# Early expert tiles: row loads without padding and release waits between them, scatters in strict turn, and a reordered hand-over

## The chip, the core and the metric

The kernel runs on one core of a Trainium2 chip. The time is that of one execution on the device, in microseconds (us); lower is better. A profile is a separate execution taken by the hardware profiler, with a span from its first to its last instruction.

## The reference

The input x is 8 sequences of 512 tokens with 256 channels, in float32. `_layernorm` is a plain normalisation over the channels, without weights.

```python
# 1: a state-space layer as a long convolution, in a residual branch
xn  = _layernorm(x)
K   = s4d_kernel(log_A_real, A_imag, C_re, C_im, log_dt, length)
y   = irfft(rfft(xn, 2*length) * rfft(K, 2*length))[:, :length]
r   = xn + y + xn * D
a   = layernorm(r) * ln_w + ln_b
x   = x + _layernorm(a)
# 2: a mixture of 8 experts, the best 2 for each token
u      = _layernorm(x)
z      = layernorm(u) * ln_g + ln_b
probs  = softmax(z @ rW + rb)
w      = top-2 of probs, divided by their sum
hid    = gelu(z @ W1[e] + b1[e])            # exact gelu, 256 -> 512
outs   = hid @ W2[e] + b2[e]                # 512 -> 256
x      = x + _layernorm(u + sum over e of outs * w[e])
```

## The kernel before

The work has three stages. In the first (0 to about 240 us) the batches go one by one through the convolution, and each token is normalised and given its two experts. In the second the 8192 token rows are worked on in 71 tiles of 128 rows. In the third (from about 519 us) the summed rows are read back, normalised and stored.

**Rows in DRAM.** For each batch GpSimd (POOL) scatters 1024 rows (`scatter`, 8 indirect DMAs) into `z_rows`, one region for each expert; a row holds its 256 values, its token number, its second expert and a logit difference. The result of a tile is weighted and added to `y_rows` by one indirect DMA that accumulates (`scatter_y(t)`); two tiles of one expert never share a token, two tiles of different experts can. So the addition of a tile may not be under way together with that of a tile of another expert.

**Early tiles.** The tiles 0 to 13 (`FIRST` = 14) take rows of the first five batches only, in the order of the experts (`first_tiles` on VectorE, DVE). Tiles 14 to 70 take the rest and begin again with expert 0; their addresses come from `count`, `share` and `tell`, which DVE runs inside the tile loop. Because the last tile of an expert reads beyond its rows, eight blocks of `zpad` are written behind the regions (`pad(e)`) before tile 14 is loaded.

**One tile.** SyncE (SP) loads the rows (`load_z`, with the address from `tab`) into `z_in`, two buffers. TensorE (PE) transposes them (`transposes`), multiplies by W1 (`first_layer`), transposes the hidden values (`turned`) and multiplies by W2 (`second_layer`). ScalarE (ACT) does `scaled`, `tilt` (a tanh), `settle`, `high`, `gelu` and `weigh`; DVE does `row`, `bias`, `low` and `output`. Each engine's order is written out by hand; in round i PE does `transposes(i+2)`, `first_layer(i+1)`, `turned(i)`, `second_layer(i-1)`. `load_z(t)` waits until tile t-2 has been transposed (`tz_mm`) and read by `row` (`dest_ready`). `yw` has six buffers, so `weigh(t)` waits for the scatter of tile t-6.

**Release.** `y_out0` and `y_out1` count the landed scatters of even and odd tiles. `scatter_y(t)` always waits for tile t-2's. For tile t-1 SP reads a number from `order`, which DVE writes in `turns`: all earlier scatters of the other parity, less one if tile t has the expert of tile t-1. SP waits for this many and raises `released`, for which POOL waits. SP does so in its one queue, between the loads:

```python
for t in range(FIRST, TILES):
    load_z(t)
    release(t - 6)
```

so `load_z(21)` stands behind `release(14)`, and in general the load of tile t+1 behind `release(t-6)`.

**The hand-over.** In the last step of stage one (`n == B`) each engine prepares tiles 0 and 1 beside the choice of experts for the last batches (`choose`, `place` on DVE; `rank`, `logits` on PE). `spin(n, bank)` is n products whose results nobody reads. The last batch is scattered by POOL ahead of `scatter_y(2)` (`EARLY` = 2).

## Time and profile before

| what | value |
|---|---|
| median of 3 runs | 565.91 us (563.12 to 567.77) |
| the profiled execution's own time | 563.68 us |
| its span | 561.6 us |
| mean granted TensorE clock | 0.93 of 2.4 GHz |
| PE, DVE, ACT, POOL busy | 80%, 79%, 67%, 48% |

Busy shares are means over stages with different limits. A timeline row gives start, length, engine, line, operation, shapes, count, and in brackets the idle time ahead of it with what ended it. PE's ends are modelled from its pipeline. Times in the rows below are us from the start of the span; tiles and their scatters are numbered from 0, and the transposes of tile 14 are those at 315.97 us.

### The profile page before, as it was taken

What the parts mean: (1) busy time and instruction counts of PE and PEld (TensorE: products, weight loads), DVE (VectorE), ACT (ScalarE), POOL (GpSimd) and SP (SyncE); (2) the same over time, 40 slices, a digit from 0 to 9 for tenths busy, and PEclk for the clock granted to TensorE, in tenths of its full rate; (3) what the DMA queues carried; (4) which work ended last, traced back from release to release, by engine and by line L of the source; (5) the groups of instructions that cost most, each with busy time, mean ns of one, the idle gap of its engine ahead of it and who ended that gap; (6) DMA issues with size and microseconds to landing.
All of it is one profiled execution on the core that took longest, in us unless ns stands there. A gap on an engine that the chain in (4) does not pass through costs nothing.

```text
span 561.6 us, 11667 instructions
## 1 busy us (share of the span) xinstructions
PE 449.8 (80%) x2730; PEld 387.5 (69%) x2730; DVE 442.2 (79%) x1492; ACT 377.1 (67%) x928; POOL 268.0 (48%) x195
## 2 busy tenths in 40 slices
PE   0296899967999978588668999999999999999100
PEld 0146888846988867257557898999999999998100
DVE  6999795999898988874858777887888878887282
ACT  6992864446666657866535777777777777776184
POOL 0000359444566877564274344445444445444365
PEclk9997999999999997688978999999999999999655
DMA  6302730042224366496245457545544444444596
GB/s 168 134 1 100 298 127 1 0 131 77 104 95 171 141 218 207 121 350 207 49 128 96 76 97 176 80 75 85 84 79 78 77 77 77 77 77 53 146 403 269
DMA packets 47615, 70.35 MB, mean 125 GB/s; under 512 B 7616, under 2 KB 37184, under 8 KB 47040
## 3 DMA queue, kind: packets, MB, share of 16 engines
q1 hardware_dynamic: 34256, 51.82, 27.7%
q0 software_dynamic: 13296, 17.80, 19.0%
q8 instruction: 26, 0.43, 0.3%
q14 instruction: 37, 0.30, 0.2%
HBM read 37.90 MB, written 31.70 MB: 124 GB/s over the span
## 4 chain that ended last, share of the span: by engine, by line
PE 47%; DVE 25%; ACT 11%; issue 6%; DMA 5%; POOL 2%; SPq 2%; another core or an unknown queue 1%; DVEq 1%; POOLq 0%; ACTq 0%
PE psum L1487 15%; PE psum L1511 14%; PE psum L1497 5%; PE psum L1407 3%; DVE ws L934 3%; DMA yr<-y_rows 2%; PE psum L1471 2%; DVE st L739 2%; PE psum L1365 2%; ACT dump L652 2%; PE psum L1354 2%; PE psum L1355 1%; DVE o L1147 1%; ACT ws L589 1%; PE psum L1378 1%
## 5 line engine op out<-in xcount | busy, mean ns | idle before, releaser
L1316 POOL DMA_INDIRECT y_rows<-yw,dst x71 | 113.0, 1591 | 141.3 <-SPq L398 86.6
L1487 PE MATMUL psum<-ws,z_hl 128*128 x426 | 121.6, 422 | 6.2 <-issue 3.2
L1511 PE MATMUL psum<-ws,h_hl 128*128 x852 | 116.4, 286 | 0.6 <-DVE h_hl L1100 0.6
L1511 PEld LDWEIGHTS psum<-ws,h_hl 128*128 128x128 f32 x852 | 104.0, 189 | 0.8 <-issue 0.8
L1487 PEld LDWEIGHTS psum<-ws,z_hl 128*128 128x128 f32 x426 | 77.7, 196 | 22.2 <-issue 8.9
L1272 POOL DMA_INDIRECT z_rows<-zn,pos x64 | 71.0, 1110 | 27.4 <-issue 17.1
L597 ACT ACTIVATE z_f<-psum,gb 128x128 f32<-128x128 f32 x142 | 57.2, 453 | 17.5 <-issue 7.5
L634 ACT ACTIVATE hg<-hb 128x512 f32<-128x512 f32 x71 | 44.9, 633 | 31.1 <-DVE hb L1094 30.1
L1407 PE MATMUL psum<-yf,it 128*128 128x256 f32 x256 | 59.2, 387 | 2.6 <-DVE r L1121 2.6
L1081 DVE CAST z_hl<-z_f 128x256 fp32r<-128x256 f32 x71 | 21.0, 296 | 48.7 <-PE psum L1487 31.9
L1378 PE MATMUL psum<-pm,ft 128*128 128x256 f32 x256 | 58.2, 382 | 0.4 <-DVE tmp L920 0.2
L627 ACT CAST h_hl<-psum 128x512 fp32r<-128x512 f32 x71 | 41.6, 585 | 24.1 <-PE psum L1497 19.4
L1407 PEld LDWEIGHTS psum<-yf,it 128*128 128x128 f32 x256 | 49.0, 194 | 9.7 <-POOL yf L1259 3.1
L1378 PEld LDWEIGHTS psum<-pm,ft 128*128 128x128 f32 x256 | 47.8, 190 | 7.2 <-issue 1.1
L1094 DVE TENSOR_TENSOR hb<-psum,b1r 128x512 f32<-128x512 f32 x71 | 48.6, 684 | 2.4 <-PE psum L1487 1.4
L1100 DVE TENSOR_TENSOR h_hl<-psum,h_hl 128x512 fp32r<-128x512 f32 x71 | 48.3, 681 | 2.3 <-ACT h_hl L627 2.0
L1497 PEld LDWEIGHTS psum<-ident,hg 128*128 128x128 f32 x284 | 36.4, 144 | 10.6 <-issue 0.6
L1497 PE MATMUL psum<-ident,hg 128*128 128x128 f32 x284 | 43.6, 277 | 0.2 <-DVE h_hl L1100 0.2
L1257 POOL TENSOR_TENSOR yf<-yf,tmp 128x512 f32<-128x512 f32 x16 | 24.4, 1525 | 39.4 <-DVE o L1147 29.6
L1265 POOL TENSOR_TENSOR pm<-xn 128x512 f32<-128x512 f32 x8 | 10.3, 1286 | 67.2 <-ACT xn L492 67.2
L607 ACT ACTIVATE yw<-y_sb,wt 128x256 f32<-128x256 f32 x71 | 35.7, 503 | 4.5 <-DVE y_sb L1111 3.2
L1471 PE MATMUL psum<-ident,z_in 128*128 128x128 f32 x142 | 27.9, 279 | 8.4 <-DMA z_in<-z_rows 4.2
(222 smaller groups left out, 841.2 us busy)
## 6 DMA issues: line engine op xcount, KB each, us to landing
z_in<-z_rows SPq DMA_DIRECT2D x71, 129.5 KB
w_raw<-in_dram SPq DMA_DIRECT2D x16, 512.0 KB, 5.9
xs<-in_dram SPq DMA_DIRECT2D x8, 512.0 KB, 5.4
x_dram<-xs SPq DMA_DIRECT2D x8, 512.0 KB
y_rows<-zn SPq DMA_DIRECT2D x8, 512.0 KB, 3.5
yr<-y_rows SPq DMA_DIRECT2D x8, 512.0 KB, 7.3
out_dram<-acc SPq DMA_DIRECT2D x7, 512.0 KB, 5.0
b1r<-in_dram SPq DMA_DIRECT2D x8, 256.0 KB
```

Source lines behind the costliest of these rows:

```text
L597: last = nc.scalar.activation(z_f[:, k], ps_z[:, k], ACT.Identity, bias=gb[:, 1, k:k + 1], scale=gb[:, 0, k:k + 1])
L627: nc.scalar.copy(h_hl[t % 2][:, 0], ps_t).then_inc(sem("h_high"), 1)
L634: nc.scalar.activation(hg[t % 2][:, :], hb[:, :], ACT.Gelu).then_inc(sem("hg_ready"), 1)
L1094: V.tensor_tensor(hb[:, :], ps_h[t % 2], b1r[:, bass.ds(e, 1)].rearrange("p a f -> p (a f)"), ALU.add).then_inc(sem("hb_ready"), 1)
L1100: V.tensor_tensor(h_hl[t % 2][:, 1], ps_t, h_hl[t % 2][:, 0].bitcast(F32), ALU.subtract).then_inc(sem("h_split"), 1)
L1272: pool.indirect_dma_start(z_rows, bass.IndirectOffsetOnAxis(ap=pos[row.par][:, i // 4, i % 4:i % 4 + 1], axis=0), zn[buf(row.b)][:, i % 4] ...
L1316: pool.indirect_dma_start(y_rows, bass.IndirectOffsetOnAxis(ap=dst[t % 8][:, 0:1], axis=0), yw[t % 6][:, :], None, compute_op=ALU.add).the ...
L1378: last = TE.matmul(fw[u][c][:, k], ft[:, c, t, kt * P:(kt + 1) * P], pm[row.b][:, c, t], start=t == 0, stop=t == 1)
L1407: last = TE.matmul(iv[c][:, j * H:(j + 1) * H], it[:, c, k, j * P:(j + 1) * P], yf[row.par][:, c, k], start=k == 0, stop=k == KT - 1)
L1487: last = TE.matmul(ps_h[q], z_hl[q][:, a, k], w_at(e, c, k * F, F), start=n == 0, stop=n == 5)
L1497: last = TE.transpose(ps_t[:, k], hg[t % 2][:, k * P:(k + 1) * P], ident[:, :])
L1511: last = TE.matmul(ps_y[q], h_hl[q][:, a, k], w_at(e, c, 1024 + k * H, H), start=n == 0, stop=n == 11)
```

## The change

Five things are edited. `release` and `pad` leave the loads of the tiles below 14: no early tile is released by SP, and the pads are issued two at a time behind the loads of tiles 9 to 12. In exchange POOL itself waits, ahead of each early scatter, until all scatters of the other parity have landed, whatever the expert. `turns` isn't run for the early tiles. ACT runs a Gelu on one number ahead of the last batch's normalisation, and `enlarge` of the last batch ahead of `gelu(0)`. PE transposes tile 1 ahead of `rank` and does six more spins; DVE splits expert 6's weights after `choose` and `row(1)`; SP loads tiles 2 and 3 earlier among the stores. The scatters take their indices from `row_of` itself, and the copy into `dst` goes.

```diff
--- before.py
+++ after.py
@@ -152,7 +152,6 @@
     tab = at("tab", [1, 2, TILES + 1], I32, c0 + 4960)
     d_rep = at("d_rep", [P, H], F32, o0 + 72 * KB)
     tab_e = at("tab_e", [P, TILES + 1], F32, c0 + 5952)
-    dst = [at(f"dst{i}", [P, 1], U32, o0 + 71 * KB + 256 + 32 * i) for i in range(8)]
     row_of = at("row_of", [P, TILES + 1], U32, o0 + 71 * KB + 736)
     half = [at(f"half{i}", [P, 1], F32, o0 + 71 * KB + 32 * i) for i in range(3)]
     lean = [at(f"lean{i}", [P, 1], F32, o0 + 71 * KB + 96 + 32 * i) for i in range(3)]
@@ -413,33 +412,34 @@
                 sp.dma_start(b1r[:, e], rep(b1[e])).then_inc(sem("in_b"), 16)
             for e in range(E):
                 sp.dma_start(b2r[:, e], rep(b2[e])).then_inc(sem("in_b"), 16)
-            store_rows(6, 7)
-            sp.wait_ge(sem("x1_ready"), B)
-            sp.dma_start(x1_dram[:, B - 1], xs[B - 1][:, :, :]).then_inc(sem("x1_stored"), 16)
-            load_z(2)
-            sp.wait_ge(sem("zn_ready"), B)
-            sp.dma_start(y_tok[:, B - 1], zn[buf(B - 1)][:, :, 0:H]).then_inc(sem(f"zn_stored{buf(B - 1)}"), 16)
-            load_z(3)
+            for b in (6, 7):
+                sp.wait_ge(sem("x1_ready"), b + 1)
+                sp.dma_start(x1_dram[:, b], xs[b][:, :, :]).then_inc(sem("x1_stored"), 16)
+                if b == 7:
+                    load_z(3)
+                sp.wait_ge(sem("zn_ready"), b + 1)
+                sp.dma_start(y_tok[:, b], zn[buf(b)][:, :, 0:H]).then_inc(sem(f"zn_stored{buf(b)}"), 16)
+                if b == 6:
+                    load_z(2)
             sp.wait_ge(sem("x1_stored"), 16 * B)
             for b in (4, 5):
                 sp.wait_ge(sem(f"scattered{buf(b)}"), sent(b))
                 sp.wait_ge(sem(f"zn_stored{buf(b)}"), sent(b) // 8)
             load_expert(sp, 7)
-            load_z(4)
-            load_z(5)
-            for t in range(6, FIRST):
+            for t in range(4, FIRST):
                 load_z(t)
-                if t > 6:
-                    release(t - 6)
-                if t == 6:
+                if t == 9:
                     sp.wait_ge(sem("pad_set"), 1)
-                pad(t - 6)
+                if 9 <= t < 13:
+                    pad(2 * (t - 9))
+                    pad(2 * (t - 9) + 1)
             sp.wait_ge(sem("pads"), 16 * E)
             for b in (5, 6, 7):
                 sp.wait_ge(sem(f"scattered{buf(b)}"), sent(b))
             for t in range(FIRST, TILES):
                 load_z(t)
-                release(t - 6)
+                if t - 6 >= FIRST:
+                    release(t - 6)
                 if 20 <= t < 23:
 
                     b = B - 1 - (t - 20)
@@ -668,6 +668,8 @@
                     measure(cur)
                 if n == B:
                     scaled(1)
+
+                    nc.scalar.activation(wt[5][:, :], eps[:, 0:1], ACT.Gelu)
                     renormalise(cur)
 
             act.wait_ge(sem("kf_mm"), 1)
@@ -682,8 +684,8 @@
             tilt(0)
             tilt(1)
             settle(0)
+            enlarge(Row(B, -1))
             gelu(0)
-            enlarge(Row(B, -1))
             for i in range(TILES + 2):
                 if i + 2 < TILES:
                     scaled(i + 2)
@@ -1018,7 +1020,6 @@
                 V.tensor_scalar(tab_e[:, 0:FIRST], tf_h[:, 0], float(E - 1), None, ALU.min)
                 do(V.scalar_tensor_tensor(tf_h[:, 2], tf_h[:, 0], float(REGION), iot[:, 1, 0:FIRST], ALU.mult, ALU.add))
                 do(V.scalar_tensor_tensor(tf_h[0:1, 3], tf_h[0:1, 1], -float(P), tf_h[0:1, 2], ALU.mult, ALU.add))
-                turns(1, FIRST, tf_h)
                 V.tensor_copy(tab[:, 0, 0:FIRST], tf_h[0:1, 3]).then_inc(sem("tab_ready"), 1)
 
             def count():
@@ -1107,7 +1108,6 @@
                 if t >= 2:
                     dve.wait_ge(sem("yw_ready"), t - 1)
                 gate(dve)
-                V.tensor_copy(dst[t % 8][:, :], row_of[:, t:t + 1])
                 V.tensor_tensor(y_sb[t % 2][:, :], ps_y[t % 2], b2r[:, bass.ds(e, 1)].rearrange("p a f -> p (a f)"),
                                 ALU.add).then_inc(sem("y_ready"), 1)
 
@@ -1169,10 +1169,10 @@
                     split_low(e)
                 if n == B:
                     row(0)
-                    split_low(6)
                     choose(tail)
                     scales_x1(cur)
                     row(1)
+                    split_low(6)
                     place(tail)
 
             statistics(0)
@@ -1305,15 +1305,18 @@
             def scatter_y(t):
 
                 q = t % 2
-                if t:
-                    pool.wait_ge(sem("released"), t)
+                if t >= FIRST:
+                    pool.wait_ge(sem("released"), t - FIRST + 1)
+                    gate(pool)
+                elif t:
+                    pool.wait_ge(sem(f"y_out{1 - q}"), ((t - 1) // 2 + 1) * 16)
                     gate(pool)
                 if t >= 2:
                     pool.wait_ge(sem(f"y_out{q}"), (t - q) * 8)
                     gate(pool)
                 pool.wait_ge(sem("yw_ready"), t + 1)
                 gate(pool)
-                pool.indirect_dma_start(y_rows, bass.IndirectOffsetOnAxis(ap=dst[t % 8][:, 0:1], axis=0),
+                pool.indirect_dma_start(y_rows, bass.IndirectOffsetOnAxis(ap=row_of[:, t:t + 1], axis=0),
                                         yw[t % 6][:, :], None, compute_op=ALU.add).then_inc(sem(f"y_out{q}"), 16)
 
             for b in range(2, B):
@@ -1536,9 +1539,10 @@
                 if tail.live:
                     logits(tail)
                 if n == B:
+                    transposes(1)
                     spin(2, 0)
                     rank(tail)
-                    transposes(1)
+                    spin(6, 0)
                     first_layer(0)
 
             for n in range(-1, B + 1):
```

POOL's queue at its first scatters of results, before. `y_rows<-yw` is `scatter_y`, `z_rows<-zn` the scatter of the last batch, and the semaphores that a row waits for are in brackets:

```order
L1316 DMA y_rows<-yw_169,dst_147 4352x256 [waits released,yw_ready]
L1272 DMA z_rows<-zn_68,pos_136 33792x259 [waits pos_ready]
L1272 DMA z_rows<-zn_68,pos_136 33792x259 x7
L1316 DMA y_rows<-yw_170,dst_148 4352x256 [waits released,y_out0,yw_ready]
L1316 DMA y_rows<-yw_171,dst_149 4352x256 [waits released,y_out1,yw_ready]
L1316 DMA y_rows<-yw_172,dst_150 4352x256 [waits released,y_out0,yw_ready]
```

The same place on POOL in the changed kernel:

```order
L1319 DMA y_rows<-yw_161,row_of 4352x256 [waits y_out0,yw_ready]
L1272 DMA z_rows<-zn_68,pos_136 33792x259 [waits pos_ready]
L1272 DMA z_rows<-zn_68,pos_136 33792x259 x7
L1319 DMA y_rows<-yw_162,row_of 4352x256 [waits y_out1,y_out0,yw_ready]
L1319 DMA y_rows<-yw_163,row_of 4352x256 [waits y_out0,y_out1,yw_ready]
L1319 DMA y_rows<-yw_164,row_of 4352x256 [waits y_out1,y_out0,yw_ready]
```

The order is the same; each early scatter now waits for both counters in full.

SP's queue from the load of tile 6 to that of tile 7, before (`TENSOR_LOAD tab` reads the address, the DMA is the load):

```order
L391 DMA z_in_186<-z_rows 128x259
L402 TENSOR_LOAD padi [waits pad_set]
L402 ISA x2
L403 ISA
L403 DMA z_rows<-zpad 128x259
L387 TENSOR_LOAD tab
L387 ISA x2
L391 ISA [waits dest_ready,tz_mm]
L391 DMA z_in_187<-z_rows 128x259
```

SP's queue from the load of tile 20 to that of tile 21 in the changed kernel:

```order
L390 DMA z_in_178<-z_rows 128x259
L395 TENSOR_LOAD order
L395 ISA x2
L446 DMA x1m<-x_dram 128x1024 [waits y_out1]
L386 TENSOR_LOAD tab
L386 ISA x2
L390 ISA [waits dest_ready,tz_mm]
L390 DMA z_in_179<-z_rows 128x259
```

Between the loads of tiles 6 and 7 the pad with its wait is gone. Between those of tiles 20 and 21 the number from `order` and the wait for `y_out1` stand in both kernels (in the changed one it is the first of its kind).

PE's queue in the hand-over from the products for the router's logits on, before:

```order
L1453 MATMUL psum<-rw_sb,zt 128x8 x8
L1427 MATMUL psum<-ident 128x512 x2
L1434 MATMUL psum<-iota_137,ident 128x32 [waits mask_ready]
L1436 MATMUL psum<-mask,upper 128x32
L1438 MATMUL psum<-mask,upper 128x24
L1438 MATMUL psum<-mask,upper 128x16
L1438 MATMUL psum<-mask,upper 128x8
L1441 MATMUL psum<-carry_b,upper 128x32 [waits carry_ready]
L1471 MATMUL psum<-ident,z_in_187 128x128 [waits zf_ready,z_in1]
L1471 MATMUL psum<-ident,z_in_187 128x128
```

and in the changed kernel:

```order
L1456 MATMUL psum<-rw_sb,zt 128x8 x8
L1474 MATMUL psum<-ident,z_in_179 128x128 [waits zf_ready,z_in1]
L1474 MATMUL psum<-ident,z_in_179 128x128
L1430 MATMUL psum<-ident 128x512 x2
L1437 MATMUL psum<-iota_137,ident 128x32 [waits mask_ready]
L1439 MATMUL psum<-mask,upper 128x32
L1441 MATMUL psum<-mask,upper 128x24
L1441 MATMUL psum<-mask,upper 128x16
L1441 MATMUL psum<-mask,upper 128x8
L1444 MATMUL psum<-carry_b,upper 128x32 [waits carry_ready]
L1430 MATMUL psum<-ident 128x512 x6
```

The transposes of tile 1 no longer stand behind the wait for `mask_ready`, and six spins lie between the ranks and the first products of tile 0.

## Rows read from the trace of the kernel before

**Rows 1.** The page: the span.

```profile
span 561.6 us, 11667 instructions
```

**Rows 2.** Busy time in stretches: start and end, length, engines, clock, DMA share, GB/s.

```profile
286.00:296.00 10.00, 5.05 (x31) 4.07 (x31) 3.52 (x17) 1.84 (x7) 7.36 (x7) 0.79 0.51 122
316.00:519.00 203.00, 202.00 (x1403) 182.84 (x1404) 162.03 (x520) 155.36 (x406) 93.29 (x60) 1.00 0.51 85
```

**Rows 3.** Timeline of PE: two spins, ranks, transposes of tiles 7 to 9, 21, 22.

```profile
243.14 1.96 PE L1427 MATMUL psum<-ident 128*128 128x512 f32 x4
247.26 0.43 PE L1434 MATMUL psum<-iota,ident 128*128 128x32 f32 x2 [2.15 <-DVE mask L959]
...
280.33 0.44 PE L1471 MATMUL psum<-ident,z_in 128*128 128x128 f32 x2 [3.17 <-DMA z_in<-z_rows]
...
286.18 0.38 PE L1471 MATMUL psum<-ident,z_in 128*128 128x128 f32 x2
...
293.75 0.66 PE L1471 MATMUL psum<-ident,z_in 128*128 128x128 f32 x2 [3.98 <-issue]
...
340.83 0.38 PE L1471 MATMUL psum<-ident,z_in 128*128 128x128 f32 x2
...
344.96 0.38 PE L1471 MATMUL psum<-ident,z_in 128*128 128x128 f32 x2
```

**Rows 4.** Timeline of DVE: `row` of tile 7, `output` of tile 4.

```profile
283.16 0.16 DVE L1067 SCALAR_TENSOR_TENSOR row_of<-z_in 128x1 uint32<-128x1 f32 x1
...
290.79 0.15 DVE L1110 COPY dst<-row_of 128x1 uint32<-128x1 uint32 x1 [4.63 <-PE psum L1511]
```

**Rows 5.** Timeline of ACT: the table load ahead of `gelu(0)`.

```profile
253.09 1.28 ACT L634 ACT_TABLE_LOAD   x1
```

**Rows 6.** Timeline of POOL: first of batch 6, scatters 0, 1, last batch, 2 to 4, 13.

```profile
251.15 0.97 POOL L1272 DMA_INDIRECT z_rows<-zn,pos  x1 [3.59 <-DVE pos L975]
...
267.60 1.61 POOL L1316 DMA_INDIRECT y_rows<-yw,dst  x1 [6.37 <-ACT yw L607]
279.56 1.57 POOL L1316 DMA_INDIRECT y_rows<-yw,dst  x1 [10.35 <-SPq L398]
281.44 1.00 POOL L1272 DMA_INDIRECT z_rows<-zn,pos  x1 [0.30 <-issue]
...
291.69 1.61 POOL L1316 DMA_INDIRECT y_rows<-yw,dst  x1 [0.31 <-issue]
293.61 1.58 POOL L1316 DMA_INDIRECT y_rows<-yw,dst  x1 [0.30 <-issue]
298.43 1.55 POOL L1316 DMA_INDIRECT y_rows<-yw,dst  x1 [3.24 <-ACT yw L607]
...
330.69 1.56 POOL L1316 DMA_INDIRECT y_rows<-yw,dst  x1 [1.22 <-DMA y_rows<-yw,dst]
```

**Rows 7.** Timeline of POOL, later scatters: 26 and 28, 60 and 61.

```profile
378.46 1.58 POOL L1316 DMA_INDIRECT y_rows<-yw,dst  x1 [3.89 <-ACT yw L607]
...
383.13 1.55 POOL L1316 DMA_INDIRECT y_rows<-yw,dst  x1 [1.20 <-DMA y_rows<-yw,dst]
...
493.94 1.59 POOL L1316 DMA_INDIRECT y_rows<-yw,dst  x1 [2.46 <-SPq L398]
499.68 1.57 POOL L1316 DMA_INDIRECT y_rows<-yw,dst  x1 [4.15 <-SPq L398]
```

**Rows 8.** Timeline of SP: behind tile 20's load, and tile 21's load.

```profile
334.84 0.33 SPq L446 DMA_DIRECT2D x1m<-x_dram  x1
335.96 0.33 SPq L391 DMA_DIRECT2D z_in<-z_rows  x1
```

**Rows 9.** The chain that ended last, landings of the loads of tiles 7 and 14.

```profile
277.72 2.57 DMA z_in<-z_rows
...
313.57 2.02 DMA z_in<-z_rows
```

**Rows 10.** What SP waited for from 268 to 314 us: total, times, longest.

```profile
SPq L402 <- DVE padi L1032: 7.2, 1, 7.2
```

## Prediction

> **What bounds the kernel now.** I read the page first: the profiled execution took 563.68 us, of which 561.6 are its span [rows 1]. The view of busy time in stretches comes next. From 316 to 519 us PE is busy 202.00 of 203.00 us at a granted clock of 1.00, DVE 182.84, ACT 162.03, POOL 93.29 [rows 2]. So from tile 14 on PE sets the time: 57 tiles in 203 us, 3.56 us each. Work taken from DVE, ACT or POOL there returns nothing; whatever makes PE idle there costs its full length, since 57 tiles of PE work wait behind it. The third view is PE's timeline, for its idle brackets: 3.17 us ahead of tile 7, 3.98 us ahead of tile 9 [rows 3], nearly none after tile 14. The fourth is POOL's queue, where the scatters of results and their waits are seen [rows 6], and the fifth what SP waited for: one wait of 7.2 us for `padi` ahead of the first pad [rows 10].
>
> **The change part by part.**
>
> *Pads and the load of tile 7.* The pad's wait holds the load of tile 7, which lands at 280.29 (277.72 + 2.57) [rows 9], and PE starts tile 7 at 280.33. That looks like 3.17 us to be won. But DVE comes to `row(7)` only at 283.16, without idle time in front: it has been working through `choose`, `place`, `count` and `share`. `gelu` and the next products need DVE's part, so PE would wait for DVE instead. An estimate for what is left of the 3.17 us is 0.25.
>
> *`dst`.* 0.15 us on DVE a tile [rows 4]. In steady state it lies beside PE: 0. In the 14 early tiles DVE is the late engine in some; an estimate is 0.5 in all.
>
> *`turns`, `release` and the pads elsewhere.* Some small DVE and SP instructions less before tile 14. Between the loads of tiles 20 and 21 nothing is saved, since `release(14)` is still there. I count 0.
>
> *Gelu and tangent.* One table load of 1.28 us [rows 5] less ahead of `gelu(0)`, but the load on one number stands ahead of the last normalisation, where ACT had idle time, and `enlarge` now stands ahead of `gelu(0)`.
>
> *The hand-over on PE.* Two spins took 1.96 us in four records, so six take 5.1 to 5.9. Ahead of the ranks PE had 2.15 us idle, waiting for `mask` [rows 3]; `mask` now comes sooner, by an estimate of 2 us, because `split_low(6)` stands behind it. Ranks at about 245.6, spins until about 251, so the first products of tile 0 start 2 to 3 us later than now, though at a higher clock perhaps. Against it, `pos` comes up to 2 us earlier, and the scatters of batch 6, which waited for it until 251.15 [rows 6]. The two ends for the first result are 2.0 us earlier and 1.6 us later; I take 0.5 earlier, near the middle.
>
> *The pause after the eight scatters of the last batch.* At 286 to 296 us the signals of PE reach the others late: DVE waits 4.63 us for products of PE [rows 4], PE idles 3.98 and its clock falls to 0.79 [rows 2, 3]. The eight scatters from 281.44 go with it. In the changed kernel they start earlier, beside `share`, and the pause may fall there. This is worth 0 to 3.5 us.
>
> The sum of the early gains is at most 0.25 + 0.5 + 0.5 + 3.5 + 0.75 (for shorter waits at tile 14 and in SP's queue, an estimate) = 5.5 us. If nothing else happened, the span would be 561.6 − 5.5 = 556.1.
>
> *The strict turn of the scatters* is the part that decides. Each early scatter now waits until all before it have landed. What such a wait costs is read where it exists today. Tile 4 has another expert than tile 3: its scatter starts at 298.43, that of tile 3 at 293.61, 4.82 apart [rows 6]. Later ones of this kind are between these and the longest, 499.68 − 493.94 = 5.74; the shortest interval that ended in a landing is 383.13 − 378.46 = 4.67 [rows 7]. ACT's result had long been there in the first (the engine named in the row isn't the releaser). I take 5.0. A tile takes 3.55 us: today scatters 2 to 13 took 330.69 − 291.69 = 39.0 us for eleven steps, because most neighbours share an expert and go side by side (293.61 − 291.69 = 1.92). So POOL's chain becomes slower than PE by 1.45 us a tile.
>
> - Scatter 0: 267.60 − 0.5 = 267.1. Scatter 1: no longer behind SP's 10.35 us wait [rows 6], + 5.0 = 272.1. The last batch: + 1.88 (281.44 − 279.56) = 274.0. Scatter 2: + 10.25 (291.69 − 281.44) = 284.2.
> - Scatters 3 to 13: 11 × 5.0 = 55.0, so scatter 13 starts at 339.2, 8.5 later than today although scatter 2 is 7.5 earlier.
> - Who waits for it? Not `weigh`: with six buffers tile 14 needs scatter 8 landed, at 319, when tile 14 has just been transposed. But SP does. Tile 14 begins again at expert 0, so `release(14)` asks for scatter 13 landed, and SP stands there between the loads of tiles 20 and 21. Today the load of tile 21 goes at 335.96 [rows 8], 5.27 after scatter 13 started; then 339.2 + 5.3 = 344.5. It lands 2.02 to 2.57 later [rows 9], I take 2.3: transposes of tile 21 at 346.8 instead of 340.83 [rows 3], **+6.0 us**. PE, which by then is up to 5.5 ahead of today, idles 6 to 11 us.
> - After idle time PE starts slowly: from one tile's transposes to the next it took 5.85 (tile 7) and 6.50 (tile 9) against 4.13 at tile 21 [rows 3]. **+2.0**.
>
> Sum: +8.0 us. All early gains are swallowed by the wait. Behind it the chain catches up, since release by expert holds again from tile 14.
>
> Here a rule of the Trainium skill speaks against my 5.0. "DMA: Bandwidth & Descriptors", in its section on the anatomy of one DMA on the gpsimd path, fits the time of one as about 2.0 us plus bytes over 436e3, which for the 131072 bytes of a tile is 2.3 us; with a small wake-up the turn would be near 3.4 us, below a tile's time, and the early gains would stay. The trace disagrees so far: no interval behind a landing is below 4.67 [rows 7].
> For the restart, "TensorE: Matmul & The Clock Gate", Part 1, says that the array is throttled by default and activity releases it; the 0.79 after the idle time agrees [rows 2].
>
> **The rivals.**
>
> 1. *The turn binds as computed*: 561.6 + 8.0 = 569.6, in this execution's terms 563.68 + 8.0 = 571.7; the median of the runs shown stands 2.2 above the profiled execution, so 573.9 by that. With 4.67 for each of twelve turns it is 4 us less, with 5.4 it is 5 more. Chance 0.55.
> 2. *It binds, but starts earlier*: beside the eight scatters of batch 6, from 251.15 on, PE's signals may come late as beside the last batch; if the reordered hand-over shrinks this, scatter 0 comes about 3 us earlier, 2.5 more than in case 1: about +5.5, 569.2 in this execution's terms and 571.4 by the median. Chance 0.15.
> 3. *It hardly binds*: a turn of 4.4 to 4.6, below every row, as a wait on POOL's own engine could be without SP's relay: within 2 us of today, 566. For it: in the rows some waits go by SP, whose queue adds a step. Against: the 4.67 is POOL's own wait for a landing. Chance 0.10.
> 4. *The other side: it doesn't bind.* If the turn is 4.0 or below, scatter 13 starts at 267.1 + 4.0 + 1.9 + 10.2 + 44 = 327.2, before today's 330.7; the load of tile 21 isn't held, and the 5.5 us stay: 558 to 561. It decides at (330.7 − 284.2 + 1.0) / 11 = 4.3 us a turn, less since PE would be earlier. Chance 0.07.
> 5. *Worse*: turns towards the 5.74 of rows 7 (+8), or PE's signals late a third time behind the idle stretch: 577 to 585. Chance 0.13.
>
> **How the numbers follow.** The likeliest is case 1, and between its two bases, 571.7 and 573.9, I take 572.8. The range must leave out at most 0.2: from 564, which holds most of case 3 and leaves case 4 out, to 580, which leaves most of case 5 out. About 1%, 5.7 us, is what a measurement of this kernel can tell from no change: between 560.3 and 571.6 counts as same. Faster: case 4, half of it a little more: 0.07. Same: case 3, nearly all of case 2 (0.12) and the lower fifth of case 1 (0.13): 0.35. Slower: 0.58.
>
> **What would show it.** On POOL the scatters 1 to 13 start at least 4.7 us apart and are released by landings, scatter 2 near 284, scatter 13 near 339. SP waits once for several microseconds for `y_rows` ahead of the load of tile 21, PE idles there 6 to 11 us and runs a stretch below clock 1.00. No load waits for `padi` at tile 7, and PE's wait there goes to DVE. From tile 22 on it is 3.56 us a tile, as now. One table load less on ACT. I am wrong if the turns are shorter than 4.3 us, if PE doesn't idle at tile 21, or if the hand-over moves the first result by more than 3 us.

## The result, and the profile after

The changed kernel takes 580.81 us (median of 4 runs, 578.04 to 582.83) against 565.73 us for the kernel before in the same set: ratio 1.0266, 95% interval 1.0205 to 1.0326. It is slower by 15 us. The direction was the forecast one; 572.8 us was forecast with a range up to 580, so the size was 8 us too small and the result lies 0.8 us outside the range.

The page of the changed kernel gives the span, 17.5 us longer than [rows 1]:

```profile
span 579.1 us, 11564 instructions
```

Busy time in stretches (start and end, length, PE, PEld, DVE, ACT, POOL busy, clock, DMA share, GB/s) of the changed kernel:

```profile
345.00:375.00 30.00, 18.70 (x118) 16.35 (x119) 12.83 (x38) 12.65 (x34) 12.48 (x8) 0.77 0.56 117
375.00:536.00 161.00, 160.88 (x1123) 145.87 (x1121) 124.62 (x367) 123.97 (x322) 73.20 (x47) 1.00 0.49 76
```

From 375 us on PE is as full as in [rows 2]. The loss lies in one place ahead of it: in 345 to 375 us PE does 18.70 us of work. PE's timeline of the changed kernel shows what it waits for. L1430 are the six spins, the first row of L1474 is tile 7, the others are tiles 20, 21 and 22:

```profile
249.65 0.41 PE L1437 MATMUL psum<-iota,ident 128*128 128x32 f32 x2 [1.88 <-DVE mask L961]
...
250.02 7.09 PE L1430 MATMUL psum<-ident 128*128 128x512 f32 x12
256.55 1.97 PE L1490 MATMUL psum<-ws,z_hl 128*128 x6
...
282.44 0.41 PE L1474 MATMUL psum<-ident,z_in 128*128 128x128 f32 x2 [0.29 <-ACT z_f L597]
...
338.60 0.38 PE L1474 MATMUL psum<-ident,z_in 128*128 128x128 f32 x2
...
356.13 0.69 PE L1474 MATMUL psum<-ident,z_in 128*128 128x128 f32 x2 [13.91 <-DMA z_in<-z_rows]
...
361.52 0.38 PE L1474 MATMUL psum<-ident,z_in 128*128 128x128 f32 x2
```

Against [rows 3]: the 3.17 us ahead of tile 7 have become 0.29, as meant. Tile 21, which had no wait, now has a wait of 13.91 us and starts at 356.13 instead of 340.83. At tile 20 the changed kernel is 1.2 us behind (338.60 against 337.38). Of the 17.5 us by which the span grew, 1.2 are there at tile 20, 14.1 arise ahead of tile 21, where the wait for one load is, and 2.2 in the restart behind it. The view of what SP waited for, 330 to 360 us (total, times, longest), names the releaser:

```profile
SPq L397 <- DMA y_rows<-yw,row_of: 16.7, 1, 16.7
```

L397 is the wait in `release(14)`. The load of tile 21 is the next but one in SP's queue. The first of these rows is the load of `x1m` (512 KB) that stands between:

```profile
350.77 0.33 SPq L446 DMA_DIRECT2D x1m<-x_dram  x1
351.89 0.33 SPq L390 DMA_DIRECT2D z_in<-z_rows  x1
```

And POOL's timeline of the changed kernel, scatters 0 and 1, the first of the last batch, scatters 2 to 6, 12 and 13, beside [rows 6]:

```profile
272.70 1.61 POOL L1319 DMA_INDIRECT y_rows<-yw,row_of  x1 [7.70 <-ACT yw L607]
278.15 1.82 POOL L1319 DMA_INDIRECT y_rows<-yw,row_of  x1 [3.84 <-DMA y_rows<-yw,row_of]
280.27 1.00 POOL L1272 DMA_INDIRECT z_rows<-zn,pos  x1 [0.30 <-issue]
...
291.13 1.61 POOL L1319 DMA_INDIRECT y_rows<-yw,row_of  x1 [0.30 <-issue]
296.09 1.58 POOL L1319 DMA_INDIRECT y_rows<-yw,row_of  x1 [3.35 <-ACT yw L607]
301.66 1.74 POOL L1319 DMA_INDIRECT y_rows<-yw,row_of  x1 [4.00 <-ACT yw L607]
307.02 1.79 POOL L1319 DMA_INDIRECT y_rows<-yw,row_of  x1 [3.63 <-DMA y_rows<-yw,row_of]
312.82 1.55 POOL L1319 DMA_INDIRECT y_rows<-yw,row_of  x1 [4.01 <-DMA y_rows<-yw,row_of]
...
342.09 1.55 POOL L1319 DMA_INDIRECT y_rows<-yw,row_of  x1 [3.27 <-DMA y_rows<-yw,row_of]
346.86 1.56 POOL L1319 DMA_INDIRECT y_rows<-yw,row_of  x1 [3.22 <-DMA y_rows<-yw,row_of]
```

No two early scatters go side by side any more. From scatter 2 to scatter 13 it takes 346.86 − 291.13 = 55.73 us, 5.07 for each turn, where it took 39.0. From scatter 1 on some rows name ACT as the releaser and some the DMA, though the turns are alike; ACT's result had been there in all of these.

The chain that ended last, asked for 320 to 362 us of the changed kernel, shows the last two links and the load that hangs on them (start, length):

```profile
342.09 3.81 DMA y_rows<-yw,row_of
...
346.86 3.82 DMA y_rows<-yw,row_of
...
351.89 4.19 DMA z_in<-z_rows
```

Scatter 12 has landed 3.81 us after its start, at 345.90, and scatter 13 starts 0.96 us later. Its landing, at 350.68, sets SP free.

### The profile page after: what moved, and what is told of

Read it like the earlier page. It is cut to its first block, busy times and chain, and to the rows that moved or that the text cites. A ratio compares the mean times of both kernels' runs of the same rounds, so it can differ in the third digit from the quotient of the medians.

```text
span 579.1 us, 11564 instructions
## 1 busy us (share of the span) xinstructions
PE 454.4 (78%) x2742; PEld 388.7 (67%) x2742; DVE 435.7 (75%) x1418; ACT 374.6 (65%) x928; POOL 263.8 (46%) x195
## 4 chain that ended last, share of the span: by engine, by line
PE 45%; DVE 22%; ACT 12%; issue 7%; DMA 6%; another core or an unknown queue 2%; POOL 2%; SPq 1%; DVEq 1%; POOLq 0%; ACTq 0%
PE psum L1490 15%; PE psum L1514 14%; PE psum L1500 4%; DMA y_rows<-yw,row_of 3%; DMA yr<-y_rows 3%; PE psum L1410 2%; PE psum L1474 2%; DVE ws L936 2%; DVE st L741 2%; PE psum L1368 2%; ACT dump L652 2%; PE psum L1357 2%; PE psum L1358 1%; ACT ws L589 1%
## 5 line engine op out<-in xcount | busy, mean ns | idle before, releaser
L1319 POOL DMA_INDIRECT y_rows<-yw,row_of x71 | 111.4, 1569 | 155.0 <-SPq L397 61.9
L1490 PE MATMUL psum<-ws,z_hl 128*128 x426 | 120.0, 418 | 6.4 <-DVE z_hl L1084 3.8
L1490 PEld LDWEIGHTS psum<-ws,z_hl 128*128 128x128 f32 x426 | 76.4, 192 | 21.9 <-issue 8.7
L1272 POOL DMA_INDIRECT z_rows<-zn,pos x64 | 68.3, 1067 | 34.8 <-issue 17.1
L1500 PE MATMUL psum<-ident,hg 128*128 128x128 f32 x284 | 43.1, 275 | 4.3 <-DVE h_hl L1101 3.7
L1500 PEld LDWEIGHTS psum<-ident,hg 128*128 128x128 f32 x284 | 35.4, 142 | 15.7 <-ACT hg L634 5.3
L1474 PE MATMUL psum<-ident,z_in 128*128 128x128 f32 x142 | 27.6, 276 | 14.2 <-DMA z_in<-z_rows 13.9
```

What stands on the lines that cost most here:

```text
L1272: pool.indirect_dma_start(z_rows, bass.IndirectOffsetOnAxis(ap=pos[row.par][:, i // 4, i % 4:i % 4 + 1], axis=0), zn[buf(row.b)][:, i % 4] ...
L1319: pool.indirect_dma_start(y_rows, bass.IndirectOffsetOnAxis(ap=row_of[:, t:t + 1], axis=0), yw[t % 6][:, :], None, compute_op=ALU.add).the ...
L1490: last = TE.matmul(ps_h[q], z_hl[q][:, a, k], w_at(e, c, k * F, F), start=n == 0, stop=n == 5)
L1500: last = TE.transpose(ps_t[:, k], hg[t % 2][:, k * P:(k + 1) * P], ident[:, :])
```

## The experiments

A remark on how to read them. The sets ran on chips on which the kernel before itself took 566.4, 559.2, 560.1 and 560.2 us. Only kernels of one set are compared in us; across sets the ratio to before stands, and even that with care, as the fourth set shows. The changed kernel itself was run beside the kernel before in the result above and in the fourth set, not in the first three.

### First set: one part alone, one part away (before: 566.36 us)

**Without the spins.** The changed kernel, and on PE:

```diff
                     rank(tail)
-                    spin(6, 0)
                     first_layer(0)
```

> The changed kernel (580.8 us) without the six spins between the ranks and the first products of tile 0. Theory (the turn of the early scatters is a chain that begins at scatter 0): in the changed kernel's profile the spins take 7.09 us and the first products start at 256.55; without them scatter 0 starts 3 to 5 us earlier, and everything down to the load of tile 21 with it: 576 to 578 us. Rival (the chain's start is set by POOL's eight scatters of batch 6 and the late signals beside them, not by PE): less than 1.5 us, 579.5 to 581.

Measured: 580.49 us (579.54 to 581.22), ratio 1.0223 [1.0182, 1.0264]. The time is in the rival's range. The ratio is 0.4% below the changed kernel's 1.0266, and the intervals overlap: what the spins cost is too small for this comparison to tell. PE's timeline of this run shows where most of their time went. In their place is a wait:

```profile
255.93 2.92 PE L1490 MATMUL psum<-ws,z_hl 128*128 x6 [3.96 <-DVE ws L936]
```

The first products of tile 0 wait for `split_low(6)`, which the change put behind `choose` and `row(1)`: `first_layer` asks for the number of experts split so far, not for its own. In the changed kernel this split ends before the spins do, so there it is the spins that hold the first products until 256.55:

```profile
251.44 2.29 DVE L936 TENSOR_TENSOR ws<-w_raw,ws 128x2048 fp32r<-128x2048 f32 x1
```

Counted from the transposes of tile 0 (245.46 in this run, 243.49 in the changed kernel) the first products start 2.6 us earlier without the spins. They then take 2.92 us instead of 1.97, behind the idle time, and scatter 0 comes 1.3 us earlier (27.93 against 29.21), not the 3 to 5 expected. The mechanism of the rival, that POOL's eight scatters set the start, isn't shown by this.

**The strict turn alone.** The kernel before, with POOL's rule for early scatters changed and the early releases gone from SP; pads, hand-over, tables and `dst` as before:

```diff
-                if t:
-                    pool.wait_ge(sem("released"), t)
+                if t >= FIRST:
+                    pool.wait_ge(sem("released"), t - FIRST + 1)
+                    gate(pool)
+                elif t:
+                    pool.wait_ge(sem(f"y_out{1 - q}"), ((t - 1) // 2 + 1) * 16)
                     gate(pool)
...
-                if t > 6:
-                    release(t - 6)
...
-                release(t - 6)
+                if t - 6 >= FIRST:
+                    release(t - 6)
```

> The kernel before (565.7 us) with one part of the change alone: POOL waits ahead of each early scatter for all landed scatters of the other parity, and SP releases none below tile 14; pads, hand-over, tables and dst as before. Theory: scatter 0 at 267.6, turns of 5.07, scatter 13 near 341, load of tile 21 near 346, its transposes near 350 instead of 340.8: 573 to 578 us, with PE idle ahead of tile 21. Rival (the hand-over's spins and reordering cost the 15 us, the turn is hidden by six buffers): 564 to 568.

Measured: 576.07 us (575.93 to 576.19), ratio 1.0151 [1.0111, 1.0191]. The turn alone makes the kernel 9.7 us slower, with the wait at tile 21 in PE's timeline and scatter 13 in POOL's at 341.38:

```profile
350.20 0.69 PE L1473 MATMUL psum<-ident,z_in 128*128 128x128 f32 x2 [6.84 <-DMA z_in<-z_rows]
```

**Everything but the strict turn.** The changed kernel with `turns(1, FIRST, tf_h)`, `release(t - 6)` behind each load from tile 7 on, and POOL's wait for `released` from tile 1 on, as before.

```diff
                 load_z(t)
+                if t > 6:
+                    release(t - 6)
                 if t == 9:
...
-                if t - 6 >= FIRST:
-                    release(t - 6)
+                release(t - 6)
```

> The changed kernel with the release by expert given back for the early tiles (turns on DVE, release on SP between the loads, POOL waits for released), all other parts of the change kept. Theory: scatter 13 comes near 330 to 334 again, no wait ahead of tile 21; the spins still delay tile 0, of which PE had made good all but about 1 us by tile 20 in the changed kernel: 564 to 569 us. Rival (the hand-over sets the time): 576 to 581.

Measured: 566.84 us (563.12 to 569.23), ratio 1.000 [0.9974, 1.0026]. All other parts of the change together are worth nothing that shows here, and without the turn the changed kernel has no loss: the turn is the cause. Tile 21 starts at 340.79 without idle time in front:

```profile
340.79 0.38 PE L1473 MATMUL psum<-ident,z_in 128*128 128x128 f32 x2
```

**Late chain, but no hold.** The changed kernel, strict turn kept, but from tile 14 on POOL itself reads its number; SP releases nothing:

```diff
+                if t == FIRST:
+                    pool.wait_ge(sem("tab_ready"), 2)
                 if t >= FIRST:
-                    pool.wait_ge(sem("released"), t - FIRST + 1)
+                    behind = pool.value_load(order[0:1, t:t + 1], min_val=16, max_val=16 * TILES)
+                    pool.wait_ge(sem(f"y_out{1 - q}"), behind)
                     gate(pool)
...
-                if t - 6 >= FIRST:
-                    release(t - 6)
...
-            for t in range(TILES - 6, TILES):
-                release(t)
```

> The changed kernel, strict turn kept for the early tiles, but from tile 14 on POOL itself reads the number from order and waits for it, so SP's queue of loads never stands behind a landing. Theory (the 14 us are lost because SP holds the load of tile 21; the late chain alone has six buffers, some 20 us, of room): PE has no long wait at tile 21 and the chain of scatters catches up: 565 to 571 us. Rival (POOL's chain is itself the bound, whoever waits): weigh waits for its buffer instead, PE idles a few tiles later, 577 to 582.

Measured: 565.57 us (560.58 to 567.71), ratio 0.9985 [0.9953, 1.0016]. In POOL's timeline of this run scatter 13, the second row, is as late as in the changed kernel:

```profile
337.99 1.62 POOL L1318 DMA_INDIRECT y_rows<-yw,row_of  x1 [3.52 <-ACT yw L603]
344.36 1.56 POOL L1318 DMA_INDIRECT y_rows<-yw,row_of  x1 [4.75 <-DMA y_rows<-yw,row_of]
```

It comes 103.48 us behind the transposes of tile 0 (240.88), in the changed kernel 103.37. Yet PE does the transposes of tile 21 without a wait:

```profile
339.56 0.38 PE L1473 MATMUL psum<-ident,z_in 128*128 128x128 f32 x2
```

A little of the rival is there too: from 345 to 365 us ACT waits for a buffer of `yw` (total, times, longest),

```profile
ACT yw L603 <- DMA y_rows<-yw,row_of: 4.7, 2, 2.5
```

and the stretch behind tile 22 is 2 to 4 us longer than in the others (220.5 us from its transposes to the end of the span, 216.6 to 218.7 there). So the six buffers nearly carry the late chain, and the time is that of the kernel before. What costs the 15 us is that SP's one queue, which also feeds PE, stands still until the chain has reached tile 13. The late chain isn't free even so: this edit also takes every other release off SP, which by itself gives 0.9903 (third set), and with early scatters by expert as well it gives 0.9887 (fourth set) against 0.9985 here. That these 1% are the late chain is likely, but the kernels did not run side by side.

### Second set: where the rest comes from (before: 559.23 us)

**The old hand-over.** The changed kernel with the hand-over of before on PE, DVE, ACT and SP put back. **DVE's and PE's order alone.** The changed kernel with only this of it put back:

```diff
-                    transposes(1)
                     spin(2, 0)
                     rank(tail)
-                    spin(6, 0)
+                    transposes(1)
                     first_layer(0)
...
                     row(0)
+                    split_low(6)
                     choose(tail)
                     scales_x1(cur)
                     row(1)
-                    split_low(6)
                     place(tail)
```

> The changed kernel with the whole hand-over of before put back (PE's and DVE's order, no six spins, no Gelu on one number, enlarge behind gelu(0), SP's loads of tiles 2 and 3); strict turn, pads and indices as changed. The turn alone on the kernel before gave 576.1, the changed kernel 580.8. Theory (the 4.7 us between them are the hand-over, which moves scatter 0 and with it the whole chain): 574.5 to 577.5, scatter 0 about 26.5 us behind the transposes of tile 0 instead of 29.2. Rival (they come from the loads and pads behind tile 4): 579.5 to 581.5.

> The changed kernel with only DVE's order (split_low(6) ahead of choose) and PE's (transposes(1) behind rank, no six spins) of the hand-over put back. Removing the spins alone changed nothing, since the first products of tile 0 then waited for split_low(6), which had been moved behind choose and row(1). Theory (that wait delays tile 0 by some 4 us): as much as the whole old hand-over gives, 575 to 578. Rival (ACT's Gelu load and SP's loads are what is late): 579.5 to 581.5.

Measured: 572.84 us, ratio 1.0259 [1.0224, 1.0294], and 573.81 us, ratio 1.0272 [1.0225, 1.0319]. The ratios are that of the changed kernel. In us both lie below the ranges of theory and rival alike, because I had written them from a chip on which the kernel before is 7 us slower, and they don't tell the theories apart. The ratio speaks for the rival in its first half (not the hand-over).

**POOL reads every number.** Pads, loads and indices as changed, old hand-over, `turns` for early tiles, and ahead of each scatter from tile 1 on:

```diff
+                if t in (1, FIRST):
+                    pool.wait_ge(sem("tab_ready"), 1 + (t == FIRST))
+                if t:
+                    behind = pool.value_load(order[0:1, t:t + 1], min_val=16, max_val=16 * TILES)
+                    pool.wait_ge(sem(f"y_out{1 - q}"), behind)
+                    gate(pool)
```

> Pads without hold, indices from row_of, old hand-over, and POOL itself reads the number from order ahead of every scatter from tile 1 on, so release by expert holds from the start and SP never stands behind a landing. Theory (with neither the late chain nor SP's hold only the small gains stay): 561 to 565. Rival (the early gains are covered by the pause beside the last batch's scatters): 565 to 568.

Measured: 553.32 us (552.31 to 555.67), ratio 0.9889 [0.9861, 0.9917]. This is faster than the kernel before, and by more than either side expected; by the ratio it is also faster than the changed kernel.

**The loads of `x1m` later.**

```diff
-                if 20 <= t < 23:
+                if 30 <= t < 33:
...
-                    b = B - 1 - (t - 20)
+                    b = B - 1 - (t - 30)
```

> The changed kernel with the three 512 KB loads of x1m, which SP issues behind tiles 20, 21 and 22, moved behind tiles 30, 31 and 32. In the changed kernel's profile one goes 1.1 us ahead of the held load of tile 21, and this load takes 4.2 us to PE instead of 2.0 to 2.6. Theory (the load shares the DMA engines with the 512 KB): 1.5 to 3 us less, 578 to 579.5. Rival (a load behind a landing takes that long anyway): 580 to 581.5.

Measured: 570.76 us, ratio 1.0223 [1.0188, 1.0258], again below both ranges. It is 2.1 us less than the changed kernel with the old hand-over in the same set, but the two intervals overlap, so the time alone doesn't show it. The trace shows the step: POOL's row of scatter 13, SP's of the load of tile 21, PE's of its transposes:

```profile
335.70 1.56 POOL L1319 DMA_INDIRECT y_rows<-yw,row_of  x1 [3.17 <-DMA y_rows<-yw,row_of]
...
340.34 4.23 SPq L390 DMA_DIRECT2D z_in<-z_rows  x3
...
342.37 0.69 PE L1474 MATMUL psum<-ident,z_in 128*128 128x128 f32 x2 [13.99 <-DMA z_in<-z_rows]
```

From scatter 13 to the transposes it takes 6.67 us; in the changed kernel it took 9.27, and between 8.40 and 9.97 in the nine other traces with this hold and the `x1m` load in front. The load itself reaches PE 2.03 us after its start instead of 4.24, and between 3.4 and 4.9 in the nine others. The theory holds in the trace: some 2 us of the wait come from the 512 KB loads around it. In the changed kernel one is issued 1.12 us ahead of it and the next 1.01 us behind it; the edit moves both, so their shares aren't told apart.

### Third set: each further part added to the turn alone (before: 560.08 us)

To the kernel with the strict turn alone came, one at a time: the pads in pairs behind the loads of tiles 9 to 12,

```diff
-            load_z(4)
-            load_z(5)
-            for t in range(6, FIRST):
+            for t in range(4, FIRST):
                 load_z(t)
-                if t == 6:
+                if t == 9:
                     sp.wait_ge(sem("pad_set"), 1)
-                pad(t - 6)
+                if 9 <= t < 13:
+                    pad(2 * (t - 9))
+                    pad(2 * (t - 9) + 1)
```

> The kernel before with the strict turn alone (earlier 1.0151 times before) and, added, the changed placing of the pads: two behind each of the loads of tiles 9 to 12 instead of one behind each of 6 to 13. In the changed kernel the three turns beside these pairs took 5.57, 5.36 and 5.80 us, with the strict turn alone 4.71 to 5.19. Theory (the pairs share the DMA engines with the scatters and lengthen turns): 1 to 2.5 us above the strict turn alone, ratio 1.017 to 1.020. Rival (the pads cost nothing, the load of tile 7 comes earlier): ratio 1.011 to 1.015.

the whole changed hand-over (its lines are those of the change's diff for PE, DVE, ACT and the stores on SP),

> The kernel before with the strict turn alone (1.0151) and, added, the whole changed hand-over (PE's and DVE's order, six spins, Gelu on one number, enlarge, SP's loads of tiles 2 and 3). Theory (the first products of tile 0 wait for split_low(6), scatter 0 comes 2 to 3 us later behind the transposes of tile 0, and the chain passes this on): ratio 1.018 to 1.022. Rival (on the chip of the second set scatter 0 came 23.6 us behind the transposes with the changed hand-over and 25.6 with the old one, so it costs nothing or gains): 1.010 to 1.016.

and the indices from `row_of`:

```diff
-                V.tensor_copy(dst[t % 8][:, :], row_of[:, t:t + 1])
...
-                pool.indirect_dma_start(y_rows, bass.IndirectOffsetOnAxis(ap=dst[t % 8][:, 0:1], axis=0),
+                pool.indirect_dma_start(y_rows, bass.IndirectOffsetOnAxis(ap=row_of[:, t:t + 1], axis=0),
```

> The kernel before with the strict turn alone (1.0151) and, added, the scatters' indices taken from row_of without the copy into dst. The column of row_of lies between other columns, 4 bytes for each partition, as a column of dst does. Theory (nothing in the chain depends on it, DVE is not the bound): ratio 1.013 to 1.017. Rival (reading indices beside columns that DVE is writing slows the scatters, turns of 5.0 instead of 4.8): 1.018 to 1.021.

Measured: 574.37 us, ratio 1.0271 [1.0206, 1.0335]; 571.66 us, 1.0235 [1.0177, 1.0293]; 573.63 us, 1.0264 [1.021, 1.0318]. All three are above what either side expected, and all alike. Three edits that each cost 1% on top of 1.0151 would cost 3% together, and the changed kernel, which has all of them, lies at 1.0266. So the base of 1.0151 was likely not that of this chip, which the fourth set tries.

**POOL reads every number, nothing else.** The kernel before with only that edit, so that SP releases nothing, neither early nor late:

> The kernel before with one change: POOL itself reads the number from order and waits for it ahead of every scatter from tile 1 on, and SP's release goes. The version with this, free pads and indices from row_of ran at 0.989 of before. Theory (SP's hold behind landings between early loads is what that version took away): ratio 0.988 to 0.994. Rival (its gain is the early load of tile 7 and the pads): 0.997 to 1.001.

Measured: 555.50 us (552.14 to 557.99), ratio 0.9903 [0.9868, 0.9938]. So the gain of the version with free pads (0.9889) is this edit, within the intervals, and not the pads. It seems to lie ahead of tile 14. In this run's trace it takes 70.02 us from the transposes of tile 0 to those of tile 14 (74.97 in the trace of before, which is from another chip), and behind tile 22 the span isn't shorter (217.96 us against 216.64). That SP's early release waits are what went is argued from this; no run took only the early ones away and left the early scatters by expert.

### Fourth set: on one chip (before: 560.24 us)

No new edits: the changed kernel, the turn alone, and POOL reading every number with the changed and with the old hand-over.

> The changed kernel as it is, on the same chip as the strict turn alone. If the parts beside the turn cost 4 us (as 580.5 against 576.1 in the first set had it), it is 3 to 6 us above the turn alone; if the difference was one of executions and chips, it is within 2 us of it, both some 13 to 15 us above the kernel before on a chip where that takes 560.

> The kernel before with the strict turn alone, beside the changed kernel on one chip. See there: 3 to 6 us below the changed kernel, or within 2 us. Its ratio to before is 1.015 if the first set's ratio holds on every chip, and 1.023 to 1.027 if the length of the chain is fixed (97 us from the transposes of tile 0 to scatter 13) while the kernel before gains on a chip with shorter waits for PE's signals.

> The changed kernel with all its parts, but POOL reads the number from order ahead of every scatter from tile 1 on (turns for the early tiles given back, no release on SP). Theory (the hand-over's parts are worth nothing where the chain doesn't bind): within 1.5 us of the same kernel with the old hand-over, both 5 to 7 us below before. Rival (the changed hand-over delays tile 0 for good): 2 to 5 us above it.

> The same with the old hand-over, which was 0.989 of before in the second set, now on one chip with the changed hand-over: ratio 0.986 to 0.992 again, and within 1.5 us of it, or 2 to 5 us below it if the changed hand-over costs.

| kernel | us | ratio to before, interval |
|---|---|---|
| changed | 572.72 | 1.0247 [1.021, 1.0284] |
| strict turn alone | 572.80 | 1.0239 [1.019, 1.0289] |
| all of the change, but POOL reads | 553.22 | 0.9887 [0.986, 0.9915] |
| the same with the old hand-over | 553.22 | 0.9891 [0.9859, 0.9924] |

Here the changed kernel and the turn alone are the same, and so are the two hand-overs. The strict turn is the whole loss on this chip. The changed kernel and the one where only POOL's rule, SP's releases and DVE's early `turns` differ are 19.5 us apart. In the latter PE does the transposes of tile 21 without a wait at 329.19, in the former at 346.43:

```profile
329.19 0.38 PE L1471 MATMUL psum<-ident,z_in 128*128 128x128 f32 x2
```

```profile
346.43 0.69 PE L1474 MATMUL psum<-ident,z_in 128*128 128x128 f32 x2 [16.93 <-DMA z_in<-z_rows]
```

On the first chip the turn alone and the changed kernel without the spins were 4.4 us apart (576.07 and 580.49). The traces give a candidate for a part of it. ACT's timeline of the changed kernel in the first profile, and of the same kernel in this set, at the same step (`high` of tile 0 behind PE's `turned`, which is the row of L1500):

```profile
266.42 0.59 ACT L627 CAST h_hl<-psum 128x512 fp32r<-128x512 f32 x1 [4.05 <-remote]
```

```profile
255.40 0.66 PE L1500 MATMUL psum<-ident,hg 128*128 128x128 f32 x4 [0.45 <-ACT hg L634]
...
256.21 0.59 ACT L627 CAST h_hl<-psum 128x512 fp32r<-128x512 f32 x1
```

In the first profile PE's row ends at 262.11 (261.45 + 0.66) and ACT goes on 4.3 us later; in the second 0.15 us later. All six traces from sets in which before takes 566 us (before, changed, and the first set) have such waits between 246 and 300 us on ACT or DVE, ended by what the timeline calls "remote" and the chain view "another core or an unknown queue", 5.8 us in all for before and 14.2 for the changed kernel; none of the twelve of the later sets has one. Scatter 0 comes 26.3 to 30.2 us behind the transposes of tile 0 in those six, and 23.3 to 28.3 in the twelve. But the waits explain at most a part: counted from the transposes of tile 0, the changed kernel's trace is 2.9 us behind that of the turn alone at scatter 0 (29.21 against 26.27), and loses another 2.8 in the eleven turns behind scatter 2 (55.73 against 52.91), where POOL waits for landings. What released these waits, and where the 4.4 us come from, stays open.

## Why the prediction was wrong in size

The sum was made for the first profile, and is checked there step by step. The mechanism of the loss was right. What failed is the size of two terms, the start of the chain and the landing of the held load.

- *Right: what bounds, and where it hits.* PE's steady state is unchanged, the wait is ahead of tile 21, on SP, for scatter 13. The turn alone and everything but the turn, run apart, gave 1.0151 (1.0239 on the chip of the fourth set) and 1.000.
- *Right: the turn.* 5.0 us was taken, 5.07 measured for the eleven turns: + 0.7 us. The lower rivals (4.4 to 4.6, and 4.0 or less) are out: the shortest of these eleven turns is 4.70. The Trainium skill, "DMA: Bandwidth & Descriptors", in its section on the anatomy of one DMA on the gpsimd path, gives about 2.3 us for a DMA of this size, by an estimate from its fit, and with that the change would have gained. The trace disagrees: 3.81 us from start to landing for scatter 12.
- *Right: the restart.* + 2.0 was taken; from tile 21 to 22 it took 5.39 instead of 4.13, and another 0.9 went behind it: 2.2 in all.
- *The step that failed first: "The two ends for the first result are 2.0 us earlier and 1.6 us later; I take 0.5 earlier".* Scatter 0 came at 272.70, 5.6 later than forecast. Of these, 2.5 arose before the hand-over: the transposes of tile 0 came at 243.49 instead of 241.00, and in all 18 traces they lie between 239.15 and 245.46 whatever the kernel, so that is a spread that the sum had no place for. The other 3.1 lie between these transposes and scatter 0: 29.21 us instead of the forecast 26.1. They are there in full at the first products of tile 0, which came 13.06 us behind the transposes where 10 was forecast. The ranks, for which `mask` was taken to come 2 us sooner, came 6.16 behind them (6.26 before), 1.6 later than forecast; six spins took 7.09 us where 5.1 to 5.9 was taken, and not the wait for `split_low(6)` but the spins ended last. By its own sign, "if the hand-over moves the first result by more than 3 us", this step was wrong. What the runs without the spins and with the old hand-over show is that mending it gives little: ratios of 1.0223 and 1.0259 against 1.0266, and on the chip of the fourth set nothing.
- *The second: "It lands 2.02 to 2.57 later".* It took 4.24 us to PE, with a 512 KB load of `x1m` just ahead and another just behind. The loads of tiles 7 and 14, from which the term was taken, have no such neighbour, and [rows 8] showed the one ahead. The step from scatter 13 to tile 21 was 9.27 us instead of 7.6: + 1.7. Moving the `x1m` loads brought this step to 6.67.
- *Small ones.* Scatter 1 came 5.45 behind scatter 0 (+ 0.45), the last batch 2.12 behind that (+ 0.24), scatter 2 10.86 behind its start (+ 0.61).

5.6 + 0.45 + 0.24 + 0.61 + 0.7 + 1.7 = 9.3 us at tile 21, and 0.2 behind it: 579.1 instead of 569.6. More than half of the miss is the position of the first link, which the prediction gave a width of 3.6 us. In a sum over a strict chain each microsecond there counts in full. The runs show this less cleanly: the eleven turns differ between traces too (52.91 to 57.26 us), for which the sum took one value. The measured time lies in the range of rival 5 (577 to 585), but not because of its turns towards 5.74; late signals may have a part in it, which no run shows.

- *"PE, which by then is up to 5.5 ahead of today"* was wrong in this trace: at tile 20 PE was 1.2 us behind, and without the turn the other parts gave 1.000. It did not spoil the sum, since a wait for the load swallows an early gain of PE: the load comes when the chain has come, and the chain isn't PE's. Why the changed kernel is 12.5 us slower than before on the chip of the fourth set and 15 in the first result wasn't tried.
- *The 14 early tiles in the kernel before* had a cost that the prediction counted as 0 ("`turns`, `release` and the pads elsewhere"). Taking all of SP's releases away gives 0.9903, and the traces put the gain ahead of tile 14.

## What to carry to other kernels

A queue that feeds the bounding engine should hold no wait for another engine's progress: here the same late chain costs 15 us if SP waits for it between loads, and gives the time of the kernel before if POOL waits for it itself. Ask of a chain of strict turns two things: what one turn costs from start to start, against the pace of the bounding engine, and at which step somebody else next asks for the chain's end. The uncertainty of such a chain's start and of its turns belongs in the range in full. And results of different chips are compared only by kernels that ran side by side, since here a ratio of 1.0151 [1.0111, 1.0191] on one chip was 1.0239 [1.019, 1.0289] on another.

## What the runs showed of the hardware

- An indirect DMA of 128 rows of 1 KB that adds into DRAM took 3.7 to 5.5 us from its start to its landing, where the chains that ended last show it in the twelve traces with the strict turn, and POOL's next one started 0.96 us after that (345.90 and 346.86 in the changed kernel). The shortest turn from scatter 2 to 13 was 4.62 us, the longest 6.90.
- A load of 128 rows took 2.03 us to PE with no 512 KB load beside it, and 4.24 when it was issued 1.12 us behind one of the same queue and 1.01 us ahead of the next.
- Between 246 and 300 us, during or up to 5 us behind the stretches in which POOL issues its series of eight scatters, ACT and DVE had idle times of 0.5 to 5.3 us that the view ends with "remote"; in one ACT went on 4.3 us after the modelled end of the PE work ahead of it, at 262.11. They were in all six traces of the sets in which before takes 566 us and in none of the twelve of those in which it takes 559 to 560. What they wait for isn't shown.
- PE's clock after the long idle time: 0.77 granted in 345 to 375 us, where PE idled 13.91 us and then worked with hardly a gap; the six products of tile 21 took 2.88 us instead of 1.65. After that it was 1.00.
